# Turning normalised activations channel-major by transposing DMAs in a conv-attention-FFN kernel

## The chip, the cores and the metric
One core of a Trainium2 chip runs the whole program. The metric is device time in microseconds (us), lower is better.

## The reference
The input is 32 images of 192 channels x 1024 positions. Three layers follow each other. Written short:

```
x = x + proj(channel_attention(qkv(x)))        # 8 heads over channels, 192x192 weights, softmax
t = tokens(x)                                  # (32, 1024, 192)
t = t + attention(layernorm(t))                # 6 heads of 32, causal, 1024 x 1024, scale 1/sqrt(192)
t = t + ffn(layernorm(t))                      # two layers, 192 -> 768 -> 192, gelu between
x = image(t)

# ffn: both layers are "bit linear": weights are the sign of (W - mean), by 5 groups of output rows, and
# the layer's output is scaled by its absolute maximum over a group of 6 images (5 groups), times 128, clipped
# to +-(128 - 1e-5). Images 30 and 31 belong to no group: their ffn output is 0.
```

The maximum over six images is why the feed-forward layer goes over a group twice: once to find the maximum, once to use it.

## The kernel before
The program is written with hand-placed semaphores, one instruction list for each engine. Images go in pairs; three pairs make a group of six (GS = 6), and there are five groups and one last pair.

**Front.** `front_part` carries an image through the first layer, the layer norm and the projections to queries, keys and values. Its steps are listed in `STEPS`: xt, g, wg, na, rb, u, mt and t (first layer), z0 to z3 (turn the normalised tokens), qk0 to qk5 and v0 to v3 (projections). A step is a few matmuls into one of two PSUM banks (`FB`) and an evacuation by ScalarE or VectorE. VectorE's layer norm pieces (`layer_norm`: stats, norm, round) are placed by `SMALL_SLOTS`. "round" writes the float16 high part of a half of the tokens (4 tiles of 128) into `zcat`, and POOL writes the low part beside it (L453, semaphore `zlo_made`). So `zcat[:, t, :]` holds, for 128 tokens, 384 float16 values: 192 high and 192 low. The projections need them with channels on the partitions, in `zt`, three blocks of 128 by 1024 tokens. `turn_z` makes this with TensorE: six 128x128 transposes for two token tiles into one PSUM bank (L595), and ScalarE copies the bank to `zt` (L809).

**Attention.** `attention` walks over slots. A slot n takes one tile of 128 queries of one head: scores on TensorE (L616, L618), their maximum on VectorE (L1082), exp on ScalarE (L841), transposes of the probabilities (L630), and later the product with the values. An image has 48 slots. Beside them the front of the next image runs: `SLOTS` says after which slot each step is issued, so z0 stands in slot 31 and qk0 in slot 35 of each image. TensorE, ScalarE and VectorE each follow this order in their own lists, so a wait in a front step holds the slots behind it. The first image's front runs alone, ahead of all attention, and the second image of the last pair has attention with no front beside it.

**SP** loads the next image once step t3 has been read, and then, after qk5, issues 16 DMAs of 192 KB (L374) that lay the high and low parts of queries and keys into `QS` and `KS`. Attention waits for these (`stacked`) at slots 0 and 24 of an image.

**Feed-forward.** `group_tail` runs after three pairs. In its first pass VectorE normalises element b+1 while element b is in work: stats, four maxima of b, norm, round, the other eight maxima (L1109). POOL makes the low parts (L472). TensorE turns them (`turn_z2`, L595, banks `ZP`), ScalarE copies them to `Z2` (`put_z2`, L862), where they stay for the second pass. Then twelve steps (`y1`, L662) multiply a half of 512 tokens by 128 output channels, ScalarE takes the absolute value (L873), VectorE the maximum. `zcat` exists once, so VectorE's round for b+1 must come after the turning of b.

## Time and profile before

| | |
|---|---|
| median of 3 runs | 5051.42 us (5050.09 to 5053.39) |
| profiled execution, its span | 5053.9 us, the time the prediction's sum is made against |
| TensorE busy | 4182.5 us, 83% |
| VectorE busy | 3623.6 us, 72% |
| ScalarE busy | 2966.6 us, 59% |
| GpSimd (POOL) busy | 773.5 us, 15% |
| DMA queue of SP | 154.38 MB, 13.0% of 16 engines' span |

The span is that of one profiled execution, from its first to its last instruction. Busy shares are averages over all stages; busy TensorE time counts modelled ends of pipelined matmuls.

### The profile page before, as it was taken

How to read it: one execution, taken by the hardware profiler on the slowest of the kernel's cores; microseconds unless marked ns; L12 is line 12 of the kernel's file. 1: busy time of each engine (PE TensorE's matmuls, PEld its weight loads, DVE VectorE, ACT ScalarE, POOL GpSimd, SP SyncE). 2: the span in 40 equal slices, each digit the busy share in tenths (PEclk: the TensorE clock that was granted, in tenths of full speed). 3: DMA queues.
4: the chain of work that ended last, by engine and by line, in shares of the span. 5: the costliest groups of instructions: out<-in, count | busy, mean ns of one | idle time of the engine just before them, and what ended most of it. 6: DMA issues, size and time to landing. Idle time of an engine off the chain costs nothing.

```text
span 5053.9 us, 119820 instructions
## 1 busy us (share of the span) xinstructions
PE 4182.5 (83%) x38848; PEld 3015.4 (60%) x38848; DVE 3623.6 (72%) x8151; ACT 2966.6 (59%) x6655; POOL 773.5 (15%) x671
## 2 busy tenths in 40 slices
PE   4989887879889876989897779889876988897777
PEld 2666664556666545666664556666545666664555
DVE  3767678767777786777778667677775777678666
ACT  1555556846555575555566746555575555566745
POOL 0000002600000143000002600000153000002600
PEclk8999998989999998999998989999998999998989
DMA  2111111011121101111111011211101111111011
GB/s 64 33 33 33 34 38 26 0 45 33 38 53 33 33 0 38 33 33 39 33 33 26 0 45 38 46 40 33 33 0 38 33 33 39 33 33 26 0 38 39
DMA packets 46393, 161.72 MB, mean 32 GB/s; under 512 B 10098, under 2 KB 10612, under 8 KB 45684
## 3 DMA queue, kind: packets, MB, share of 16 engines
q1 hardware_dynamic: 45812, 154.38, 13.0%
q8 instruction: 315, 5.16, 0.4%
q14 instruction: 266, 2.18, 0.1%
HBM read 28.52 MB, written 25.17 MB: 11 GB/s over the span
## 4 chain that ended last, share of the span: by engine, by line
issue 78%; POOL 13%; PE 5%; DVE 2%; POOLq 1%; ACT 0%; DMA 0%; SPq 0%; DVEq 0%; ACTq 0%
POOL work L483 7%; POOL hi_z L453 1%; POOL hi_z L472 1%; POOL rstd L448 1%; POOL rstd L468 1%; PE S L662 1%; POOL NK L443 1%; PE OUT L649 1%; PE PT L734 1%; PE PT L630 1%; DVE nmax L1082 0%; PE S L670 0%; DVE work L339 0%; DMA B<-in_b 0%; PE S L616 0%
## 5 line engine op out<-in xcount | busy, mean ns | idle before, releaser
L841 ACT ACTIVATE work<-S,nmax 128x128 f32<-128x128 f32 (+7 forms) x1536 | 1138.8, 742 | 1119.0 <-DVE nmax L1082 1112.1
L1082 DVE TENSOR_REDUCE nmax<-S 128x1 f32<-128x128 f32 (+7 forms) x1536 | 1155.4, 753 | 620.3 <-PE S L618 574.5
L630 PE MATMUL PT<-ident,work 128*128 128x128 f32 x6912 | 1089.2, 282 | 270.5 <-DVE work L339 246.9
L630 PEld LDWEIGHTS PT<-ident,work 128*128 128x128 f32 x6912 | 752.4, 142 | 493.6 <-DVE work L339 291.5
L339 DVE COPY work<-PT 128x512 f32<-128x512 f32 (+3 forms) x1536 | 893.1, 581 | 25.1 <-PE PT L630 19.4
L662 PE MATMUL S<-odd,W1b 128*128 (+1 forms) x2160 | 526.9, 400 | 71.4 <-DVE work L1155 64.1
L483 POOL TENSOR_TENSOR work<-work 128x512 f16<-128x512 f32 x360 | 414.0, 1158 | 148.4 <-ACT work L887 120.1
L662 PEld LDWEIGHTS S<-odd,W1b 128*128 128x128 f16 x2160 | 214.1, 102 | 354.4 <-DVE work L1155 94.8
L616 PE MATMUL S<-KS,QS 128*128 128x512 f16 (+3 forms) x1152 | 335.9, 347 | 103.5 <-issue 60.9
L443 POOL TENSOR_TENSOR NK<-NK,halfneg 96x4 f32<-96x4 f32 x32 | 32.5, 1016 | 2200.7 <-DVE NK L1007 2200.7
L845 ACT ACTIVATE work<-PT 128x512 f32<-128x512 f32 (+3 forms) x768 | 330.3, 430 | 57.1 <-PE PT L630 57.1
L618 PE MATMUL S<-causal,identb 128*128 128x128 bf16 x1536 | 343.9, 224 | 0.0
L616 PE MATMUL S<-odd 128*128 128x512 f16 (+3 forms) x1152 | 315.1, 328 | 9.9 <-ACT work L841 7.1
L895 ACT ACTIVATE work<-work,sc 128x512 f32<-128x512 f32 x360 | 285.7, 801 | 60.9 <-DVE work L1155 60.6
L649 PE MATMUL OUT<-work,odd 128*32 128x128 f32 x6912 | 310.0, 279 | 7.6 <-ACT oT L833 7.6
L649 PE MATMUL OUT<-work,V 128*32 128x128 f32 x6912 | 306.8, 278 | 0.0
L734 PE MATMUL PT<-W2b,work 128*128 128x192 f16 x2880 | 259.5, 252 | 56.0 <-POOL work L483 56.0
L841 ACT ACTIVATION_READ_ACCUMULATOR work<-S,nmax 128x1 f32 x1536 | 299.4, 195 | 0.0
L734 PEld LDWEIGHTS PT<-W2b,work 128*128 128x128 f16 x2880 | 246.9, 101 | 79.2 <-POOL work L483 54.9
L1155 DVE TENSOR_SCALAR work<-S,sc 128x512 f32<-128x512 f32 x360 | 266.5, 801 | 21.6 <-POOL work L483 14.8
L649 PEld LDWEIGHTS OUT<-work,odd 128*32 128x32 f32 x6912 | 239.7, 111 | 51.5 <-issue 33.2
L649 PEld LDWEIGHTS OUT<-work,V 128*32 128x32 f32 x6912 | 237.1, 110 | 41.4 <-issue 33.4
(189 smaller groups left out, 6718.5 us busy)
## 6 DMA issues: line engine op xcount, KB each, us to landing
X<-in_x SPq DMA_DIRECT2D x32, 768.0 KB, 5.3
odd<-hi_z SPq DMA_DIRECT2D x128, 192.0 KB, 4.1
odd<-odd SPq DMA_DIRECT2D x128, 192.0 KB, 4.2
out_y<-work SPq DMA_DIRECT2D x64, 384.0 KB, 3.1
QS<-hi_z SPq DMA_DIRECT2D x64, 192.0 KB, 3.5
QS<-odd SPq DMA_DIRECT2D x64, 192.0 KB, 4.0
KS<-hi_z SPq DMA_DIRECT2D x64, 192.0 KB, 4.6
KS<-odd SPq DMA_DIRECT2D x64, 192.0 KB, 4.5
```

The lines of the kernel that those rows point to most:

```text
L339: copy(PTS[m % 2][:, m // 2 % RING, P * c0:P * (c0 + k)], PT[i % 2][:, 0:P * k]).then_inc(pt_free[i % 2], 1)
L483: pool.tensor_tensor(hs[:, 1, :], H[:, i % MH, :], hs[:, 0, :], ALU.subtract).then_inc(hlo_made, 1)
L616: mm(S[:, n % 2, c0:min(w, c0 + 512)], q, KS[u][:, h, c0:min(w, c0 + 512)], start=True, stop=c0 + 512 < w)
L618: mm(S[:, n % 2, w - P:w], identb[:, :], causal[:, :], start=False, stop=True).then_inc(scores_full, 1)
L630: last = tr(bank[:, P * (j - c0):P * (j - c0) + P], PS[m % 2][:, m // 2 % 2, P * j:P * j + P], ident[:, :])
L649: last = mm(OUT[32 * hh:32 * hh + 32, 0:P], V[u][:, j, D * h:D * h + D], PTS[k % 2][:, unit_of(k, hh) // 2 % RING, P * j:P * j + P], start ...
L662: last = mm(bank, W1b[:, j, P * (i % 6):P * (i % 6) + P], rhs[:, j, :], start=(j == 0), stop=(j == 2))
L734: last = mm(PT[tp % 2][:, C * t:C * t + C], HS[:, hf, part, m, o:o + P], W2b[:, m, :], start=(m == 0 and part == 0), stop=(m == MH - 1 and ...
L841: A(PS[n % 2][:, n // 2 % 2, 0:w], S[:, n % 2, 0:w], ACT.Exp, bias=nmax[:, n:n + 1], accum_out=rowsum[:, n:n + 1]).then_inc(exp_made, 1)
L845: pt_copy(act, lambda o, x: A(o, x, ACT.Copy), pair, i)
L895: A(h, h, ACT.Gelu, bias=rb1[:, i % 6:i % 6 + 1], scale=r1).then_inc(gelu_made, 1)
L1082: v.tensor_reduce(nmax[:, n:n + 1], S[:, n % 2, 0:P * (qtile(n) + 1)], AX.X, ALU.max, negate=True).then_inc(max_made, 1)
```

## The change
The steps z0 to z3 are dropped, with `turn_z`, `turn_z2`, `put_z2` and the float16 identity. Instead SP issues `dma_start_transpose` for each tile of 128 tokens, from `zcat` to `zt` in the front and to `Z2` in the feed-forward, eight per image, in two halves of four that each wait for POOL's low part. A half has its own semaphore (`z_turned`, `z2_turned`), which reaches 64 for each image. TensorE waits for it at qk0 and qk1, and at y1's steps 0 and 6. VectorE waits for both halves ahead of the next element's norm, and its stats no longer wait. The projections and layer norm pieces get other slots: qk and v one later, the layer norm's up to one and a half earlier. `abs_made` starts at 4, which shifts the counts in its waits by 4 and keeps what they stand for.

```diff
--- before.py
+++ after.py
@@ -92,14 +92,14 @@
 
 
 STEPS = ["xt0", "xt1", "xt2", "xt3", "g0", "g1", "wg0", "wg1", "na", "rb", "u", "mt", "t0", "t1", "t2", "t3",
-         "z0", "z1", "z2", "z3", "qk0", "qk1", "qk2", "qk3", "qk4", "qk5", "v0", "v1", "v2", "v3"]
+         "qk0", "qk1", "qk2", "qk3", "qk4", "qk5", "v0", "v1", "v2", "v3"]
 FREES = {"wg0": 2, "wg1": 2, "mt": 2}
 LN_PER = 26
 JR = 8
 XSOFT = 9
 FRONT_STEPS = len(STEPS)
 
-NEEDS = {"g0": "xt3", "wg0": "g1", "na": "wg1", "mt": "u", "t0": "mt", "qk0": "z3"}
+NEEDS = {"g0": "xt3", "wg0": "g1", "na": "wg1", "mt": "u", "t0": "mt"}
 
 
 def bank_of(step):
@@ -118,12 +118,11 @@
 
 
 SLOTS = {"xt0": 0, "xt1": 1, "xt2": 2, "xt3": 4, "g0a": 5, "g0": 6, "g1a": 7, "g1": 8, "wg0": 9, "wg1": 10,
-         "na": 11, "rb": 15, "u": 18, "mt": 19, "t0": 20, "t1": 21, "t2": 22, "t3": 23, "z0": 31, "z1": 32,
-         "z2": 33, "z3": 34, "qk0": 35, "qk1": 36, "qk2": 37, "qk3": 38, "qk4": 39, "qk5": 40, "v0": 41, "v1": 42,
-         "v2": 43, "v3": 44}
-
-SMALL_SLOTS = {"norms": 12, "rdiag": 13, "logits": 16, "xexp": 17, "attn": 17.5, "ln_stats0": 22, "ln_stats1": 25,
-               "ln_norm0": 27, "ln_norm1": 28, "ln_round0": 28.5, "ln_round1": 29}
+         "na": 11, "rb": 15, "u": 18, "mt": 19, "t0": 20, "t1": 21, "t2": 22, "t3": 23, "qk0": 36, "qk1": 37,
+         "qk2": 38, "qk3": 39, "qk4": 40, "qk5": 41, "v0": 42, "v1": 43, "v2": 44, "v3": 45}
+
+SMALL_SLOTS = {"norms": 12, "rdiag": 13, "logits": 16, "xexp": 17, "attn": 17.5, "ln_stats0": 22, "ln_stats1": 24,
+               "ln_norm0": 26, "ln_norm1": 26.5, "ln_round0": 27, "ln_round1": 27.5}
 
 
 def hybrid_kernel(nc, x, wa, wb, wv, wpt, bp, temp, w3, w1, b1, w2, b2, out):
@@ -141,7 +140,6 @@
 
 
         ident = sb("ident", [P, P])
-        ident16 = sb("ident16", [P, P], F16)
         identb = sb("identb", [P, P], BF16)
         causal = sb("causal", [P, P], BF16)
         ones = sb("ones", [CH + 1, CH])
@@ -240,7 +238,6 @@
         FR = ctx.enter_context(nc.psum_tensor("FR", [P, 512], F32))
         FB = [FR[:, :], S[:, 0, 512:1024]]
         Y = [S[:, i // 2, 512 * (i % 2):512 * (i % 2) + 512] for i in range(4)]
-        ZP = [FR[:, :], OUT[:, :]]
 
 
         w_in = sem("w_in")
@@ -259,6 +256,7 @@
         ln_step = sem("ln_step")
         rstd_made = sem("rstd_made")
         zlo_made = sem("zlo_made")
+        z_turned = [sem(f"z_turned{i}") for i in range(2)]
         qkhi_made = sem("qkhi_made")
         qklo_made = sem("qklo_made")
         stacked = [sem(f"stacked{i}") for i in range(2)]
@@ -273,8 +271,7 @@
         ln2_step = sem("ln2_step")
         rstd2_made = sem("rstd2_made")
         z2lo_made = sem("z2lo_made")
-        z2t_full = sem("z2t_full")
-        z2t_made = sem("z2t_made")
+        z2_turned = [sem(f"z2_turned{i}") for i in range(2)]
         y1_full = sem("y1_full")
         abs_made = sem("abs_made")
         max1_step = sem("max1_step")
@@ -366,6 +363,11 @@
                     sp.wait_ge(front_full, after(pair, u, FRONT_STEPS, STEPS.index("t3") + 1))
                     load_x(pair * 2 + (u + 1))
 
+                for hf in range(2):
+                    sp.wait_ge(zlo_made, after(pair, u, 2, hf + 1))
+                    alone(sp)
+                    for t in range(4 * hf, 4 * hf + 4):
+                        sp.dma_start_transpose(zt[:, :, P * t:P * t + P], zcat[:, t, :]).then_inc(z_turned[hf], 16)
 
                 sp.wait_ge(qklo_made, after(pair, u, 6, 6))
                 for grp in range(2):
@@ -389,6 +391,13 @@
                     front(pair, u + 1, True)
 
             def group_tail(g):
+                with sp.Fori(0, GS) as b:
+                    for hf in range(2):
+                        sp.wait_ge(z2lo_made, g * (2 * GS) + b * 2 + (hf + 1))
+                        alone(sp)
+                        for t in range(4):
+                            sp.dma_start_transpose(Z2[:, b, hf, :, P * t:P * t + P],
+                                                   zcat[:, 4 * hf + t, :]).then_inc(z2_turned[hf], 16)
                 with sp.Fori(0, GS) as b:
                     for hf in range(2):
                         store(g * GS + b, hf, g * (2 * GS) + b * 2 + (hf + 3))
@@ -426,7 +435,6 @@
             pool.wait_ge(cst_made, 11)
             pool.affine_select(out=bm, in_=bm, compare_op=ALU.is_ge, fill=MASKED, base=XD - 1,
                                pattern=[[0, 2], [XD, CH // XD], [0, XD]], channel_multiplier=-1).then_inc(cst_made, 1)
-            pool.tensor_copy(ident16[:, :], ident[:, :]).then_inc(cst_made, 1)
             pool.tensor_copy(identb[:, :], ident[:, :]).then_inc(cst_made, 1)
 
             pool.wait_ge(prep, 3)
@@ -493,7 +501,7 @@
         def _(pe):
             mm = nc.tensor.matmul
             tr = nc.tensor.transpose
-            pe.wait_ge(cst_made, 14)
+            pe.wait_ge(cst_made, 13)
             pe.wait_ge(w_in, 16 * 10)
             pe.wait_ge(w_ready, 1)
 
@@ -565,14 +573,11 @@
                         cols = slice((2 * k + t) * P, (2 * k + t + 1) * P)
                         mm(FR[:, C * t:C * t + C], X[0:CH + 1, 0, cols], MT[0:CH + 1, 0, :], start=True, stop=False)
                         last = mm(FR[:, C * t:C * t + C], X[0:CH, 1, cols], MT[0:CH, 1, :], start=False, stop=True)
-                elif name[0] == "z":
-                    k = int(name[1:])
-                    if k % 2 == 0:
-                        pe.wait_ge(zlo_made, after(pair, u, 2, k // 2 + 1))
-                    last = turn_z(FR, k)
                 elif name.startswith("qk"):
                     i = int(name[2:])
                     m, hf = i // 2, i % 2
+                    if m == 0:
+                        pe.wait_ge(z_turned[hf], after(pair, u, 64, 64))
                     for j in range(3):
                         for w in (W3h, W3l):
                             last = mm(FR, w[:, j, P * m:P * m + P], zt[:, j, 512 * hf:512 * hf + 512],
@@ -586,14 +591,6 @@
                                           w[:, j, 2 * C:3 * C], start=(j == 0 and w is W3h),
                                           stop=(j == 2 and w is W3l))
                 last.then_inc(front_full, 1)
-
-            def turn_z(bank, k):
-
-                v = bank.bitcast(F16).rearrange("p (j n) -> p j n", j=4)
-                for t in range(2):
-                    for j in range(3):
-                        last = tr(v[:, j, P * t:P * t + P], zcat[:, 2 * k + t, P * j:P * j + P], ident16[:, :])
-                return last
 
             pe.sem_inc(ot_full, 2)
             pe.sem_inc(y2_full, 4)
@@ -683,34 +680,16 @@
                     pe.wait_ge(st, nb * (GS * STACKS) + STACKS)
                 alone(pe)
 
-                def turn_z2(ab, abs_before):
-                    for k in range(4):
-                        if k % 2 == 0:
-                            pe.wait_ge(z2lo_made, ab * 2 + (k // 2 + 1))
-                        if k >= 2:
-                            pe.wait_ge(z2t_made, ab * 4 + (k - 1))
-                        turn_z(ZP[k % 2], k).then_inc(z2t_full, 1)
-                    if abs_before is not None:
-
-                        pe.wait_ge(abs_made, abs_before)
-                        alone(pe)
-
                 def y1(b, ab):
                     for i in range(12):
                         if i % 6 == 0:
-                            pe.wait_ge(z2t_made, ab * 4 + (2 + 2 * (i // 6)))
-                        if i >= 4:
-                            pe.wait_ge(abs_made, ab * 12 + (i - 3))
+                            pe.wait_ge(z2_turned[i // 6], ab * 64 + 64)
+                        pe.wait_ge(abs_made, ab * 12 + (i + 1))
                         ffn1(Z2[:, b, i // 6], Y[i % 4], i).then_inc(y1_full, 1)
 
-
-                turn_z2(g * GS, None)
-                with pe.Fori(0, GS - 1) as b:
-                    ab = pe.snap(g * GS + b)
-                    y1(b, ab)
-                    turn_z2(pe.snap(ab + 1), ab * 12 + 12)
-                y1(GS - 1, g * GS + (GS - 1))
-                pe.wait_ge(abs_made, nb * (GS * 12))
+                with pe.Fori(0, GS) as b:
+                    y1(b, pe.snap(g * GS + b))
+                pe.wait_ge(abs_made, nb * (GS * 12) + 4)
                 alone(pe)
 
                 def y(b, ab, hf, clips):
@@ -771,6 +750,7 @@
             act.wait_ge(w_ready, 1)
             act.sem_inc(os_made, 2)
             act.sem_inc(hlo_made, MH)
+            act.sem_inc(abs_made, 4)
 
             def front_part(name, pair, u):
                 f = u % 2
@@ -803,10 +783,6 @@
                 elif name[0] == "t":
                     k = int(name[1:])
                     o = A(T0[:, f, 2 * k:2 * k + 2, :], FR[:, 0:2 * C].rearrange("p (a b) -> p a b", a=2), ACT.Copy)
-                elif name[0] == "z":
-                    k = int(name[1:])
-                    v = FR.bitcast(F16).rearrange("p (j n) -> p j n", j=4)
-                    o = A(zt[:, :, 256 * k:256 * k + 256], v[:, 0:3, :], ACT.Copy)
                 elif name.startswith("qk"):
                     i = int(name[2:])
                     A(QKH[:, i // 2, 512 * (i % 2):512 * (i % 2) + 512], FR, ACT.Copy,
@@ -854,14 +830,6 @@
 
             def group_tail(g):
 
-                def put_z2(b, ab):
-                    for k in range(4):
-                        act.wait_ge(z2t_full, ab * 4 + (k + 1))
-                        alone(act)
-                        zv = ZP[k % 2].bitcast(F16).rearrange("p (j n) -> p j n", j=4)
-                        A(Z2[:, b, k // 2, :, 256 * (k % 2):256 * (k % 2) + 256], zv[:, 0:3, :],
-                          ACT.Copy).then_inc(z2t_made, 1)
-
                 def abs_y1(ab):
                     for i in range(12):
                         act.wait_ge(y1_full, ab * 12 + (i + 1))
@@ -872,12 +840,8 @@
                             act.wait_ge(max1_step, ab * 14 + g + (i - JR + 2))
                         A(JUNK[:, i % JR, :], Y[i % 4], ACT.Abs, bias=B1[:, i % 6:i % 6 + 1]).then_inc(abs_made, 1)
 
-                put_z2(0, g * GS)
-                with act.Fori(0, GS - 1) as b:
-                    ab = act.snap(g * GS + b)
-                    abs_y1(ab)
-                    put_z2(act.snap(b + 1), act.snap(ab + 1))
-                abs_y1(g * GS + (GS - 1))
+                with act.Fori(0, GS) as b:
+                    abs_y1(act.snap(g * GS + b))
 
                 def split_h(ab, i):
                     act.wait_ge(gelu_made, ab * 12 + (i + 1))
@@ -966,7 +930,7 @@
                     link(v.scalar_tensor_tensor(out=wbin[:, :, cols], in0=wf[:, :, cols], scalar=means[:, g:g + 1],
                                                 in1=wc[:, :, cols], op0=ALU.is_gt, op1=ALU.subtract))
             dve.wait_ge(prep_all, 3)
-            dve.wait_ge(cst_made, 14)
+            dve.wait_ge(cst_made, 13)
             dve.wait_ge(bias_in, 16)
             v.memset(X[CH:CH + 1, 0, :], 1.0).then_inc(w_ready, 1)
 
@@ -1105,7 +1069,7 @@
 
                 def max_y1(ab, first, last):
                     for i in range(first, last):
-                        dve.wait_ge(abs_made, ab * 12 + (i + 1))
+                        dve.wait_ge(abs_made, ab * 12 + (i + 5))
                         v.tensor_reduce(gm[:, i:i + 1], JUNK[:, i % JR, :], AX.X, ALU.max).then_inc(max1_step, 1)
                     if last == 12:
                         base = ab * 14 + (g + 1)
@@ -1121,10 +1085,11 @@
                     ab = dve.snap(g * GS + b)
                     b1, ab1 = dve.snap(b + 1), dve.snap(ab + 1)
 
-                    dve.wait_ge(z2t_full, ab * 4 + 4)
-                    alone(dve)
                     norm2(b1, ab1, "stats", range(TT))
                     max_y1(ab, 0, 4)
+                    for hf in range(2):
+                        dve.wait_ge(z2_turned[hf], ab * 64 + 64)
+                        alone(dve)
                     norm2(b1, ab1, "norm", range(TT))
                     norm2(b1, ab1, "round", halves[0])
                     norm2(b1, ab1, "round", halves[1])
```

## Rows read from the trace of the kernel before
**Rows 1.** Page, part 1: busy us (share of the span) and instructions of each engine.
```profile
PE 4182.5 (83%) x38848; PEld 3015.4 (60%) x38848; DVE 3623.6 (72%) x8151; ACT 2966.6 (59%) x6655; POOL 773.5 (15%) x671
```

**Rows 2.** Windows: start:end, length, busy time (x instructions) of each engine, PEclk, DMA share, GB/s.
```profile
4910.80:4921.32 10.52, 9.85 (x120) 7.26 (x121) 7.26 (x17) 8.70 (x20) 0.82 (x1) 1.00 0.01 2
5003.14:5012.61 9.47, 7.94 (x94) 5.68 (x95) 7.18 (x18) 6.08 (x16) 0.00 (x0) 1.00 0.01 2
298.70:306.60 7.90, 7.55 (x108) 5.96 (x108) 5.86 (x13) 7.34 (x16) 0.10 (x1) 1.00 0.01 2
283.50:298.70 15.20, 10.29 (x108) 6.77 (x106) 14.39 (x39) 7.60 (x22) 4.92 (x4) 1.00 0.19 53
835.22:849.27 14.05, 11.09 (x60) 5.29 (x60) 13.52 (x41) 9.98 (x15) 5.23 (x5) 0.88 0.00 0
```

**Rows 3.** Timeline of a front in attention: start us, us, engine, line, work.
```profile
293.89 0.55 DVE L991 CAST hi_z<-XT 128x768 f16<-128x768 f32 x1
...
294.53 1.59 POOL L453 TENSOR_TENSOR hi_z<-XT,hi_z 128x768 f16<-128x768 f32 x1 [3.80 <-DVE hi_z L991]
...
298.78 0.51 PE L595 MATMUL FR<-ident,hi_z 128*128 128x128 f16 x6
...
300.09 0.80 ACT L809 ACTIVATE zt<-FR 128x768 f16<-128x768 f16 x1
...
306.79 0.38 PE L578 MATMUL FR<-zt,W3h 128*128 128x512 f16 x1
```

**Rows 4.** Timeline of the first feed-forward pass, one element to the next.
```profile
835.22 3.39 POOL L472 TENSOR_TENSOR hi_z<-XT,hi_z 128x768 f16<-128x768 f32 x2 [3.27 <-DVE hi_z L991]
...
837.11 0.51 PE L595 MATMUL FR<-ident,hi_z 128*128 128x128 f16 x6 [2.92 <-POOL hi_z L472]
...
840.24 9.27 PE L662 MATMUL S<-odd,W1b 128*128 x36
...
841.87 0.69 ACT L873 ACTIVATE work<-S,B 128x512 f32<-128x512 f32 x1 [0.76 <-PE S L662]
...
843.01 7.30 ACT L873 ACTIVATE work<-S,B 128x512 f32<-128x512 f32 x11 [0.45 <-PE S L662]
...
846.32 2.40 DVE L986 TENSOR_SCALAR XT<-T,mv,rstd 128x192 f32 x8
...
849.27 1.84 POOL L472 TENSOR_TENSOR hi_z<-XT,hi_z 128x768 f16<-128x768 f32 x1 [3.27 <-DVE hi_z L991]
```

**Rows 5.** Timeline of POOL and VectorE: first and last element of a group.
```profile
807.52 3.38 POOL L472 TENSOR_TENSOR hi_z<-XT,hi_z 128x768 f16<-128x768 f32 x2 [2.99 <-DVE hi_z L991]
...
877.37 3.39 POOL L472 TENSOR_TENSOR hi_z<-XT,hi_z 128x768 f16<-128x768 f32 x2 [3.27 <-DVE hi_z L991]
...
884.54 7.96 DVE L1109 TENSOR_REDUCE gm<-work 128x1 f32<-128x512 f32 x12 [1.64 <-ACT work L873]
```

**Rows 6.** Timeline of the first front, alone ahead of attention.
```profile
91.77 3.38 POOL L453 TENSOR_TENSOR hi_z<-XT,hi_z 128x768 f16<-128x768 f32 x2 [2.99 <-DVE hi_z L991]
...
100.48 0.63 PE L578 MATMUL S<-zt,W3h 128*128 128x512 f16 x1
```

**Rows 7.** Timeline of SP: first and last stack DMAs, then the next front's first.
```profile
215.85 0.51 SPq L374 DMA_DIRECT2D odd<-hi_z  x1
...
221.91 0.89 SPq L374 DMA_DIRECT2D odd<-hi_z  x1
...
227.32 2.23 SPq L374 DMA_DIRECT2D odd<-odd  x2
...
324.37 0.52 SPq L374 DMA_DIRECT2D QS<-hi_z  x1
```

**Rows 8.** The stack DMAs from hi_z: duration ns min/median/max, and landing us.
```profile
L374 SPq DMA_DIRECT2D odd<-hi_z x128: 513/889/1832, 215.9 to 4947.5; - x128
...
DMA to landing us min/median/max: 2.6/4.2/5.0
```

**Rows 9.** Timeline of TensorE: first scores of slot 48.
```profile
227.26 0.22 PE L616 MATMUL S<-odd 128*128 128x128 f16 x1
```

## Prediction

> **What bounds the kernel now.** I read the page first. TensorE is busy 83% of the span and VectorE 72% [rows 1], an average over two kinds of stage, so the windows come next. In attention with a front running beside it, the stretch that holds the steps z0 to z3 keeps TensorE busy 7.55 and ScalarE 7.34 of 7.90 us, while the layer norm stretch before it is VectorE's (14.39 of 15.20 us) [rows 2]. Work taken from TensorE and ScalarE can therefore pay, but only in the z stretch. The first feed-forward pass, an element of the batch at a time, has VectorE busy 13.52 of 14.05 us [rows 2]: there the reader is to see that neither the PE transposes nor the ScalarE copies set the pace. The timeline shows why: POOL starts the low part of an element's first half at 835.22, TensorE turns it at 837.11, the first feed-forward matmul starts at 840.24, and the next element's low part starts at 849.27 [rows 4].
>
> **Removed.** Per front four steps of six transposes (a group spans 0.51 us on TensorE) and four copies of 0.80 us [rows 3], together 2.0 us of TensorE and 3.2 us of ScalarE, in 32 fronts, of which 31 lie inside attention. What that is worth there I read from the same five slots, 31 to 35, in the last pair: 10.52 us beside a front, 9.47 us where there is none [rows 2]. The 1.05 us between them is all that z0 to z3 and most of qk0 cost, since VectorE's score maxima keep their pace (7.26 against 7.18 us busy). qk0 moves to slot 36 and takes its share with it. Ends: nothing, and the whole 2.0 us of TensorE if the stretch were TensorE's alone. I take 0.8, nearer to the measured pair: 31 x 0.8 = 25 us gained (0 to 62). In the feed-forward pass the same removal gains nothing by itself, as VectorE is the bound; what counts there is the new latency. The dropped identity copy at the start of the program is hidden by the weight loads and costs or gains nothing. The layer norm pieces run one to one and a half slots earlier within VectorE's full stretch: the same work in another order, nothing.
>
> **Added.** Eight transposing DMAs per element, each turning 128 tokens x 384 values (98 KB), issued by SP, four per half, each half after its zlo_made or z2lo_made. Their price is not in this trace. Call d the time from one to the next, and L that from the issue of the last to its landing. The nearest rows are the sixteen stack DMAs of a front: issued from 215.85 to 229.55, 0.86 us each, 192 KB each, the shortest 0.51 us on the queue [rows 7]; they land 2.6 us (shortest) to 4.2 us (median) after issue [rows 8]. A transposing DMA has half the bytes but, in blocks of 128, 384 destination runs of 256 B against 96 of 2 KB. By bytes it would take 0.43 us, which the shortest issue lifts to 0.51; by runs 4 x 0.86 = 3.4; and 4.2 if one had to land before the next. I take twice the stack DMA's pace, d = 1.7, and L = 3.0, as they find the DMA engines empty (DMA share 0.01 [rows 2]). Ends: d 0.51 and 4.2, L 2.6 and 4.2.
>
> The Trainium skill ("VectorE: DVE Perf Modes", The three transpose paths) gives 1309 ns for a 128x128 bf16 block turned by DMA and 390 ns by TensorE; three blocks a DMA would make d an estimated 3.9 and the total about 6100 us. The same skill ("DMA: Bandwidth & Descriptors", Latency and other measured facts) has transposing DMAs at 261 GB/s, by which 98 KB is an estimated 0.38 us of data, and the sum would be near that of the lower end. The rows can't decide between them, as none here transposes by DMA.
>
> **Feed-forward pass, 5 groups of 6 elements.** Counted from the start of an element's first low part: it is ready after 1.84 us [rows 4], its first half is turned at t0 = 1.84 + 3d + L, its second at t1 = 1.84 + 7d + L. zcat has one buffer, and VectorE now waits for both halves before it normalises the next element; ahead of that wait stand four maxima that need the first half's matmuls. From first matmul to the fourth maximum, as now: 840.24, first ScalarE pass 841.87, the next eleven 0.66 apart from 843.01, plus 0.68 for the maximum, 5.5 us [rows 4, 5]. From the start of the normalising to the next low part 2.95 us (846.32 to 849.27) [rows 4]. The period is
> max(t0 + 5.5, t1 + 0.1) + 2.95.
> With d = 1.7 and L = 3.0: t0 = 9.94, t1 = 16.74, period 19.8. Now five periods take 69.85 us (807.52 to 877.37) [rows 5]; after, 99.0. Loss per group 29.1. The last element ends now 15.1 us after its low part begins (877.37 to 884.54 + 7.96) [rows 5]; after, it waits for its second half, then six steps and maxima, 6.2 us: 22.9, a loss of 7.8. Five groups: 5 x 36.9 = 185 us. VectorE's own 13.5 us fits into 19.8; queued behind its wait are the norm, the rounding and eight maxima, so ScalarE and TensorE stand too.
>
> **Attention.** A unit of 48 slots takes 108.5 us (215.85 to 324.37) [rows 7], 2.26 us a slot. Now rounding starts at 293.89 in slot 28.5 and qk0 at 306.79 in slot 35 [rows 3], 12.9 us. After, it is slot 27 to 36, 2.5 slots more, less the 0.8 saved: 17.7 us, and 20.0 to qk1, which needs the second half. Needed from the rounding: 0.64 + 1.59 [rows 3] + 7d + L = 17.1 for qk1, 10.3 for qk0. Both are hidden by the attention of slots 27 to 36; without that cover they would cost their full length. They stay hidden up to d = 2.1. Above it TensorE stands at qk1 with the next scores queued behind it, and VectorE and ScalarE wait for those: 7(d - 2.1) us per front. On SP the stack DMAs come one slot later: now their first half is issued by 221.9 and lands by some 226, and the first scores of slot 48 start at 227.26 [rows 7, 8, 9]. The margin of about 1 us shrinks; 0 to 1 us in 16 units, I take nothing. X's load goes out ahead of the transposes and waits for nothing new.
>
> **The first front** has no cover: from its low part (91.77) to qk1 (100.48) 8.7 us [rows 6]; after, t1 = 16.7, 8 us lost once.
>
> **Sum.** 185 + 8 - 25 = +168 us on the profiled execution's 5053.9 us; that is 2.5 above the median, so from 5051.4: **5219 us**.
>
> **The rivals.**
> (a) Forecast: d from 1.0 to 2.1, hidden in attention, exposed in the feed-forward pass. At d = 1.0 the sum is +54 (5105), at 2.1 +255 (5306). Chance 0.50. For it: VectorE's full loop and the single zcat.
> (b) The transposing DMA is dear, d above 2.1, and holds up attention too. At 2.8: feed-forward +416, first front +16, stalls 31 x 4.9 = 152, less 25: 5610. For it: four times the runs of a stack DMA. Against: half the bytes. Chance 0.17.
> (e) The transposing DMAs do not overlap at all, each waiting for the landing of the one before: d = 4.2 as in [rows 8]. Period 37.3, feed-forward +710, first front +26, stalls 31 x 14.7 = 456, less 25: 6220. Against: the stack DMAs overlap fourfold on the same queue. Chance 0.10. The Trainium skill's 1309 ns a block ("VectorE: DVE Perf Modes", The three transpose paths) would bring the kernel close to this case; no run here shows it yet.
> (c) Faster: the DMAs cost little and the removed work pays more. At d = 0.51 and L = 2.6 the period is 14.4, the last element 16.7, the feed-forward loss 19 us, the first front even; with 0.8 a front the sum is -6, with 2.0 it is -43 (5008). It decides from a gain of 0.6 us a front at that d; at d = 1.0 it would need 2.5, more than the 2.0 that TensorE gives up. For it: the DMA engines are idle. Against: L alone puts 2.6 us where TensorE and ScalarE needed little. Chance 0.12.
> (d) The same balance within 0.2% (10 us), about what a measurement of this kernel can tell from no change: 0.06. The rest, 0.05, goes to losses below (a)'s, d between 0.6 and 1.0.
>
> The range of (a) alone is 5105 to 5306. To hold eight in ten it reaches down into (d) and up to d = 2.8 in (b), and leaves out (e): 5040 to 5610. Faster 0.12, same 0.06, slower 0.82.
>
> **What would show it.** In the first feed-forward pass the low parts on POOL should stand about 20 us apart, with VectorE's XT line waiting for a DMA; SP's transposes give d directly. The wait at the first qk matmuls should stay small; if it is long, (b) holds. Slots 31 to 35 beside a front should come near 9.5 us. The prediction fails if d is far from 1.7, each 0.1 us of it above 1.3 being worth some 21 us, or if transposing DMAs slow the engines' own reads.

## Result: slower by 2.9%, and the profile after

| | before | after |
|---|---|---|
| median | 5052.41 us (5050.09 to 5057.66) | 5198.86 us (5194.31 to 5210.00) |
| ratio, 95% interval | | 1.0293 [1.0278, 1.0308] |
| span of the profiled execution | 5053.9 us | 5194.1 us, 140.2 more |

Times and ratios, here and below, are of fast executions alone: one of experiment 7 (5763.14 us) and one of the kernel before beside experiment 12 (9008.38 us) were slow and are left out.

The page of the changed kernel, part 1 and two lines on its DMAs (packets; the queue SP's DMAs use, with its share of 16 engines' span):

```profile
PE 4112.8 (79%) x37360; PEld 2940.9 (57%) x37360; DVE 3632.8 (70%) x8151; ACT 2791.3 (54%) x6407; POOL 778.8 (15%) x670
...
DMA packets 252727, 210.52 MB, mean 41 GB/s; under 512 B 216434, under 2 KB 216948, under 8 KB 252020
...
q1 hardware_dynamic: 252148, 203.21, 17.5%
```

TensorE and ScalarE have lost the work as intended (ScalarE 2966.6 to 2791.3 us against [rows 1]), yet the span is longer. The transposes bring 206,000 packets under 512 B, but the queue's share is only 17.5%. The engines idle more, so the question is what they wait for.

**The price of a transposing DMA.** Timelines of SP (start, length of the whole burst, count) in the first front and in the feed-forward pass, then the instructions by line (duration in ns min/median/max) with the time from issue to landing:

```profile
93.73 10.38 SPq L370 DMA_TRANSPOSE zt<-hi_z  x8
...
840.39 10.53 SPq L399 DMA_TRANSPOSE odd<-hi_z  x8
```

```profile
L370 SPq DMA_TRANSPOSE zt<-hi_z x256: 1177/1257/2645, 93.7 to 5056.5; - x128
...
L399 SPq DMA_TRANSPOSE odd<-hi_z x240: 1177/1178/1858, 822.9 to 4802.3; - x120
...
DMA to landing us min/median/max: 2.3/2.3/3.6
```

Eight take 10.4 to 10.5 us, so d is 1.30 to 1.32 us (forecast 1.7), and L is 2.3 to 2.4 us (forecast 3.0).

**Feed-forward pass**, one element to the next, timeline of all engines; the answer to [rows 4]:

```profile
838.36 3.38 POOL L480 TENSOR_TENSOR hi_z<-XT,hi_z 128x768 f16<-128x768 f32 x2 [12.23 <-DVE hi_z L955]
...
846.96 9.42 PE L659 MATMUL S<-odd,W1b 128*128 x36 [7.50 <-DMA odd<-hi_z]
...
850.46 2.11 DVE L1073 TENSOR_REDUCE gm<-work 128x1 f32<-128x512 f32 x3 [0.46 <-ACT work L841]
...
852.48 2.40 DVE L950 TENSOR_SCALAR XT<-T,mv,rstd 128x192 f32 x8
...
855.43 3.39 POOL L480 TENSOR_TENSOR hi_z<-XT,hi_z 128x768 f16<-128x768 f32 x2 [6.45 <-DVE hi_z L955]
```

From the low part (838.36) to the first matmul (846.96) are 8.60 us where there were 5.02; the matmuls had waited 7.50 us for the DMA. The fourth maximum ends as the normalising starts (852.48), and 2.95 us later POOL starts the next element. The period is 17.07 us. POOL's first and last element of the group, the answer to [rows 5], and the waits of TensorE for these DMAs in the whole kernel (us in total, times, longest):

```profile
820.87 3.38 POOL L480 TENSOR_TENSOR hi_z<-XT,hi_z 128x768 f16<-128x768 f32 x2 [2.99 <-DVE hi_z L955]
...
906.57 3.39 POOL L480 TENSOR_TENSOR hi_z<-XT,hi_z 128x768 f16<-128x768 f32 x2 [6.47 <-DVE hi_z L955]
```

```profile
PE S L659 <- DMA odd<-hi_z: 278.7, 31, 17.8
```

VectorE, which has a wait of its own for the second half ahead of the normalising, stands there for a DMA once in the whole kernel (from the list of who waited for L399: us, times):

```profile
  DVE XT L950: 0.2, 1
```

So the loop is set by TensorE's wait for the first half and the four maxima behind it, and not by the second half.

Five periods take 85.70 us (69.85 before), and the last element, to 926.1, takes 19.5 us (15.1 before): 20.3 us a group. The whole stretch from a group's last score maximum to the next group's first, by windows, the five stretches summed (first number; then busy time of each engine), is this before and after:

```profile
sum 1368.60, PE 974.17 PEld 619.01 DVE 974.01 ACT 886.58 POOL 574.62; mean PE 194.83 PEld 123.80 DVE 194.80 ACT 177.32 POOL 114.92
```

```profile
sum 1470.56, PE 921.16 PEld 567.52 DVE 981.64 ACT 799.02 POOL 573.79; mean PE 184.23 PEld 113.50 DVE 196.33 ACT 159.80 POOL 114.76
```

That is 102 us more, with VectorE's busy time unchanged (974 and 982): of 140.2 us the largest part is there. Below, this sum is called the group tails. Nearly all of it lies in the first pass: from a group's first low part to its last maximum the five groups together take 526.4 us, where they took 425.6.

**Attention.** The third pair of images by windows that run from one score maximum to another: slot 0, slots 24 to 30 (layer norm), 31 to 35, slot 48 (the second image's first) and slots 72 to 78 (the second image's layer norm). Before, then after:

```profile
575.69:577.31 1.62, 1.62 (x9) 1.06 (x9) 0.29 (x2) 0.84 (x3) 0.00 (x0) 0.50 0.05 15
630.10:644.82 14.72, 9.93 (x106) 6.55 (x104) 13.87 (x38) 7.03 (x22) 4.20 (x4) 1.00 0.22 55
644.82:655.35 10.53, 9.78 (x120) 7.28 (x121) 7.28 (x17) 8.71 (x20) 0.83 (x1) 1.00 0.01 3
683.35:684.24 0.89, 0.85 (x8) 0.39 (x5) 0.89 (x4) 0.49 (x3) 0.00 (x0) 1.00 1.06 221
738.49:752.98 14.49, 9.90 (x106) 6.54 (x104) 13.68 (x39) 7.03 (x22) 4.21 (x4) 1.00 0.22 56
```

```profile
585.91:589.50 3.59, 1.48 (x7) 0.93 (x7) 0.29 (x2) 0.95 (x3) 0.00 (x0) 0.50 0.01 2
642.60:657.77 15.17, 10.95 (x106) 7.14 (x104) 13.84 (x39) 7.14 (x22) 5.24 (x4) 0.89 0.29 66
657.77:667.34 9.57, 8.06 (x95) 5.76 (x96) 7.19 (x17) 6.08 (x16) 0.00 (x0) 1.00 0.33 64
695.76:697.19 1.43, 1.43 (x13) 1.04 (x12) 0.99 (x3) 1.02 (x4) 0.00 (x0) 1.00 0.88 193
751.43:767.34 15.91, 10.92 (x106) 7.41 (x104) 13.84 (x38) 7.23 (x22) 5.22 (x4) 0.89 0.24 58
```

Slots 31 to 35 fall by 0.96 us, as hoped. But slot 0 takes 3.59 instead of 1.62, the layer norm stretches 15.17 and 15.91 instead of 14.72 and 14.49, at a granted clock of 0.89 instead of 1.00, and slot 48 takes 1.43 instead of 0.89. Averaged over the first fifteen pairs (from the start times of the maxima) the first image of a pair takes 110.19 us instead of 108.52 and the second 105.54 instead of 105.09. Over the kernel attention loses about 30 us instead of gaining 25. Three places are to be explained.

*Layer norm.* VectorE and TensorE of the changed kernel in the second image, by timeline, and a window of 2 us in it:

```profile
752.57 1.13 DVE L942 BATCH_NORM_STATS2 stats<-T 128x6 f32<-128x192 f32 x4
753.62 0.41 DVE L946 BATCH_NORM_AGGREGATE mv<-stats 128x2 f32<-128x6 f32 x4
753.95 1.23 DVE L1046 TENSOR_REDUCE nmax<-S 128x1 f32<-128x1024 f32 x1
...
757.37 2.40 DVE L950 TENSOR_SCALAR XT<-T,mv,rstd 128x192 f32<-128x192 f32 x8
...
755.83 0.77 PE L627 MATMUL PT<-ident,work 128*128 128x128 f32 x5 [2.26 <-DVE work L336]
...
761.15 1.12 PE L627 MATMUL PT<-ident,work 128*128 128x128 f32 x4 [2.28 <-DVE work L336]
```

```profile
761.50:763.50 2.00, 2.00 (x11) 0.90 (x9) 1.46 (x5) 1.58 (x5) 1.86 (x2) 0.50 0.02 4
```

Two things have changed in VectorE's order. The second half's statistics (1.13 and 0.41 us), one slot earlier now, stand ahead of a long maximum of 1.23 us. And both halves of the normalising are one piece of 2.40 us, since the new slots 26 and 26.5 meet, again with a long maximum behind it. VectorE's evacuation of the transposed probabilities comes late behind each, and TensorE waits 2.26 and then 2.28 us. After the second wait the granted clock is 0.50, the lower of its two levels (1.2 GHz), in the window from 761.50. In the kernel before the statistics stood ahead of a short maximum, the normalising in two pieces of 1.24 us, and the longest wait of TensorE in that stretch was 1.03 us:

```profile
743.32 0.41 DVE L982 BATCH_NORM_AGGREGATE mv<-stats 128x2 f32<-128x6 f32 x4
743.65 0.29 DVE L1082 TENSOR_REDUCE nmax<-S 128x1 f32<-128x128 f32 x1
...
745.78 1.24 DVE L986 TENSOR_SCALAR XT<-T,mv,rstd 128x192 f32<-128x192 f32 x4
...
750.92 1.06 PE L630 MATMUL PT<-ident,work 128*128 128x128 f32 x8 [1.03 <-DVE work L339]
```

*Slot 48.* Its first scores wait for the stack DMAs ("idle before" in brackets):

```profile
695.45 0.23 PE L613 MATMUL S<-odd 128*128 128x128 f16 x1 [0.82 <-DMA odd<-odd]
```

*Slot 0.* TensorE at the head of the third pair, then the waits of that kind in the whole kernel:

```profile
585.52 0.37 PE L528 MATMUL FR<-ident,X 96*128 96x96 f32 x1
588.02 0.32 PE L527 MATMUL FR<-ident,X 97*128 97x97 f32 x1 [2.13 <-issue]
```

```profile
PE FR L527 <- issue: 29.3, 14, 2.4
```

Between two steps of the front TensorE stands 2.13 us and waits for nothing that the profile shows ("issue"). It does so at 14 of 16 pair heads, 29.3 us in all. The kernel before has no such row: there L519 follows itself without a gap. (Another "issue" wait, ahead of a pair's first scores, is in both kernels, 60.9 us before and 60.8 us after at 14 pairs, and explains no difference.)

### The profile page after: what moved, and what is told of

Its sections match the earlier page's. It is cut to its first block, busy times and chain, and to the rows that moved or that the text cites. A ratio compares the mean times of both kernels' runs of the same rounds, so it can differ in the third digit from the quotient of the medians.

```text
span 5194.1 us, 117149 instructions
## 1 busy us (share of the span) xinstructions
PE 4112.8 (79%) x37360; PEld 2940.9 (57%) x37360; DVE 3632.8 (70%) x8151; ACT 2791.3 (54%) x6407; POOL 778.8 (15%) x670
## 3 DMA queue, kind: packets, MB, share of 16 engines
q1 hardware_dynamic: 252148, 203.21, 17.5%
## 4 chain that ended last, share of the span: by engine, by line
issue 79%; POOL 12%; PE 5%; DVE 2%; DMA 1%; POOLq 1%; SPq 0%; ACT 0%; DVEq 0%; ACTq 0%
POOL work L491 7%; POOL hi_z L461 1%; POOL hi_z L480 1%; POOL rstd L456 1%; POOL rstd L476 1%; PE S L659 1%; PE OUT L646 1%; POOL NK L451 1%; PE PT L627 1%; PE PT L713 1%; DVE nmax L1046 0%; PE S L667 0%; SPq L399 0%; DVE work L336 0%; PE S L613 0%
## 5 line engine op out<-in xcount | busy, mean ns | idle before, releaser
L627 PE MATMUL PT<-ident,work 128*128 128x128 f32 x6912 | 1104.0, 284 | 286.0 <-DVE work L336 271.7
L659 PE MATMUL S<-odd,W1b 128*128 (+1 forms) x2160 | 545.5, 410 | 350.4 <-DMA odd<-hi_z 278.7
L613 PE MATMUL S<-KS,QS 128*128 128x512 f16 (+3 forms) x1152 | 340.8, 352 | 97.2 <-issue 60.8
L841 ACT ACTIVATE work<-S,B 128x512 f32<-128x512 f32 x360 | 238.4, 687 | 332.6 <-PE S L659 329.3
L1073 DVE TENSOR_REDUCE gm<-work 128x1 f32<-128x512 f32 x360 | 228.1, 680 | 131.8 <-ACT work L841 130.3
```

What stands on the lines that cost most here:

```text
L613: mm(S[:, n % 2, c0:min(w, c0 + 512)], q, KS[u][:, h, c0:min(w, c0 + 512)], start=True, stop=c0 + 512 < w)
L627: last = tr(bank[:, P * (j - c0):P * (j - c0) + P], PS[m % 2][:, m // 2 % 2, P * j:P * j + P], ident[:, :])
L659: last = mm(bank, W1b[:, j, P * (i % 6):P * (i % 6) + P], rhs[:, j, :], start=(j == 0), stop=(j == 2))
```

## Experiments

The ratios are to the kernel before, measured in turn with it. The edits are shown shortened: "..." marks what is left out, semaphore counts are left out too, and the comments in them are mine.

**1. The front alone** (feed-forward pass as before) and **2. the feed-forward pass alone** (front as before). Edits: the hunks of the diff for the one part, the other left out.

> The front's transposes go by DMA with the changed slots, the feed-forward pass keeps TensorE and ScalarE. Theory A (the loss is the sum of two stages: 102 us in the five feed-forward gaps, 5 us in the first front, some 33 us in attention): 5052 + 38 = 5090 us. Theory B (attention loses only because the feed-forward pass hands its images over late or with a slow TensorE clock): 5052 + 5 - 25 = 5032 us.

Measured: 5090.77 us, ratio 1.0074 [1.0058, 1.0091]; group tails 1374.9 us, images 110.00 and 105.45 us.

> Only the feed-forward pass turns by DMA, the front is the old one. Theory A: 5052 + 102 = 5154 us, low parts on POOL 17.1 us apart, pairs as long as before. Theory B: some 33 us more, 5187 us, as the pairs grow with it.

Measured: 5155.90 us, ratio 1.0204 [1.0187, 1.0221]; group tails 1469.5 us, images 108.31 and 105.07 us. The parts add up (39 + 104 us, against the 146 us of both together), and the front costs time though it was meant to save it.

**3. The layer norm's and projections' old slots.**

```diff
-SLOTS = {..., "qk0": 36, "qk1": 37, ..., "v3": 45}
+SLOTS = {..., "qk0": 35, "qk1": 36, ..., "v3": 44}
-"ln_stats1": 24, "ln_norm0": 26, "ln_norm1": 26.5, "ln_round0": 27, "ln_round1": 27.5
+"ln_stats1": 25, "ln_norm0": 27, "ln_norm1": 28, "ln_round0": 28.5, "ln_round1": 29
```

> The changed kernel with the layer norm pieces back in the slots of before and qk and v one slot earlier again. Theory A1 (attention loses by the new slots: 0.7 to 1.0 us a unit in slots 24 to 30, and 0.6 to 0.8 us at slot 48, where the scores wait for late stack DMAs): slots 24 to 30 back at 14.6 us, no wait at slot 48, 26 + 11 us gained, 5199 - 37 = 5162 us. Theory A2 (the transposing DMAs in flight slow the engines, whatever the slots): no gain, or a loss of up to 2 us a front where qk1 now waits for its half, 5199 to 5260 us.

Measured: 5187.07 us, ratio 1.0262 [1.0245, 1.0279]. Slots 24 to 30 are back at 14.76 and 14.49 us and slot 48 at 0.95, as expected. The total is not, 25 us above theory A1: qk0 in slot 35 gives back 0.6 us of each 0.96, TensorE waits at qk1 for the second half's DMAs in five images (6.9 us in all), and the group tails are 13 us longer (1483.5), though nothing was edited there. Of these 13, 5 lie in the first pass (531.8 against 526.4) and 6 behind it. That part I can't explain.

**4. Code moved.** 64 instructions without work on TensorE's list, ahead of its loop over the groups; nothing else.

```diff
+            for _ in range(64):
+                alone(pe)
             groups(pe, pair_body, group_tail)
```

> The changed kernel with 64 semaphore increments more on TensorE, once, ahead of its loops: no work in any loop changes, only where the loop's instructions lie in memory. Theory C (the 2.0 us more in the first slot of each pair are a wait for TensorE's instructions, set by where the code lies): the first slot's 3.6 us change, to some 1.5 us or to more, and the whole by up to 15 x 2 = 30 us either way. Theory D (the wait has to do with the changed work): nothing changes, 5199 us.

Measured: 5175.53 us, ratio 1.0240 [1.0223, 1.0257]. Slot 0 falls from 3.55 to 1.57 us on average; slots 24 to 30 rise by 0.4 to 0.5 us. The 64 instructions run once, ahead of the loop, so what changes inside it is only where TensorE's code lies, and the wait at slot 0 depends on that. The 0.4 to 0.5 us given back in slots 24 to 30 are not explained.

**5. Two buffers in the feed-forward pass.** `zt` is free there and serves as a second `zcat`. VectorE normalises an element ahead, and its wait is for the transposes of the element before last. With the buffer VectorE's order changes too: the normalising moves ahead of the four maxima, and the loops over elements are written out.

```diff
+        zcat2 = [zcat, zt[:, :, :].rearrange(...)]
...
-                            sp.dma_start_transpose(Z2[...], zcat[:, 4 * hf + t, :])
+                            sp.dma_start_transpose(Z2[...], zcat2[b % 2][:, 4 * hf + t, :])
...
+                norm2(0, ..., "stats"); normalise(0); norm2(1, ..., "stats")
+                for b in range(GS):
+                    if b + 1 < GS: normalise(b + 1)       # waits for the transposes of b - 1
+                    max_y1(b, 0, 4)
+                    if b + 2 < GS: norm2(b + 2, ..., "stats")
+                    max_y1(b, 4, 12)
```

> The changed kernel with a second zcat (in zt, idle in the feed-forward pass), VectorE normalising element b+1 ahead of the maxima of b, and only waiting for the turning of b-1. Theory A (the 102 us are the DMAs' latency inside VectorE's loop, not their work): the loop falls back to VectorE's own 13.6 us a period, the last element ends some 8 us after its first maximum; 105 us per group become 80, 5199 - 5 x 25 = 5074 us. Theory B (eight transposing DMAs and their SP issue are a bound of their own, or slow the engines): period near 17 us stays, no gain over 20 us.

Measured: 5100.10 us, ratio 1.0097 [1.0080, 1.0114]. The group tails fall from 1470.6 to 1378.8 us, 92 us of the 125 expected, and the whole kernel stays 26 us above the expectation. POOL's third and sixth element of a group in this kernel:

```profile
847.78 3.38 POOL L482 TENSOR_TENSOR hi_z<-XT,hi_z 128x768 f16<-128x768 f32 x2 [6.44 <-DVE hi_z L957]
...
889.12 3.39 POOL L482 TENSOR_TENSOR zt<-XT,zt 128x768 f16<-128x768 f32 x2 [6.36 <-DVE zt L957]
```

The period is 13.8 us ((889.12 - 847.78) / 3), a little under the 13.97 of before, with the same eight DMAs an element. From first low part to last maximum the five groups take 427.9 us, against 526.4 in the changed kernel and 425.6 before. So what the DMAs cost in the changed kernel was latency in a loop with one buffer, and neither SP's time nor the transfers. A group's first element still waits uncovered, but the 10 us by which the tails stay above those of before lie mostly behind the first pass (8 us), and no run says why.

**6. The same with the layer norm's old slots** (third and fourth line of experiment 3's diff alone).

> As the pipelined kernel, and the layer norm pieces in the slots of before (qk and v stay one slot later). Slots 24 to 30 back to 14.6 us and 31 to 35 at 9.57, so 0.7 to 1.0 us a unit less than the pipelined one: 5074 - 26 = 5048 us, level with before's 5052 or just under it. If the layer norm slots were not the cause in attention, 5074 us.

Measured: 5084.99 us, ratio 1.0063 [1.0046, 1.0080], 15 us less than experiment 5 and 37 more than expected: the 26 of experiment 5, gaps between the pairs that grew by 6.6 us, and group tails that grew by 4.8. The layer norm stretch of the last pair (slots 24 to 30), after and in this kernel:

```profile
5034.39:5050.48 16.09, 10.96 (x106) 7.40 (x104) 13.80 (x39) 7.21 (x22) 5.28 (x4) 0.89 0.07 13
```

```profile
4929.80:4944.04 14.24, 9.82 (x106) 6.50 (x104) 13.70 (x39) 7.02 (x22) 4.25 (x4) 1.00 0.04 7
```

1.85 us less, clock 1.00: the slots of the layer norm alone bring the stretch back, while the projections keep their later ones. The clock itself seems to cost little there: in experiment 9 below, slots 24 to 30 of the third pair have 0.88 and take 14.82 us. So it is mostly the waits that cost. The experiment moves all the pieces back at once, so it does not tell the merged normalising from the statistics ahead of a long maximum.

**7. One DMA of twelve blocks a half** in place of four of three, and **8. one block a DMA**, both with the single `zcat`. In 7 `Z2` is laid out by token tiles and TensorE reads it in four pieces of 128.

```diff
-                        for t in range(4):
-                            sp.dma_start_transpose(Z2[:, b, hf, :, P * t:P * t + P], zcat[:, 4 * hf + t, :])
+                        sp.dma_start_transpose(Z2[:, b, hf, :, :, :].rearrange("p t j n -> p (t j) n"),   # 7
+                                               zcat[:, 4 * hf:4 * hf + 4, :])
...
+                            for j in range(3):                                                           # 8
+                                sp.dma_start_transpose(Z2[:, b, hf, j, P * t:P * t + P],
+                                                       zcat[:, 4 * hf + t, P * j:P * j + P])
```

> The changed kernel with one transposing DMA for each half in the feed-forward pass (12 blocks of 128x128) in place of four of 3 blocks; Z2 is laid out so that its output is contiguous, and the matmuls read it in four runs of 128. Theory A (SP pays by block, 0.43 us): a half still takes 5.2 us and lands 2.4 us later at most, period 17 us or up to 1 us more, 5199 us or up to 25 more. Theory B (SP pays by instruction, some 1.2 us): a half lands within 3 us, the period falls to VectorE's 14 us, 5199 - 90 = 5109 us.

> The changed kernel with three transposing DMAs of one 128x128 block each in place of one of three blocks, in the feed-forward pass. Theory A (by block): SP issues one in 0.43 us, 1.3 us a tile of tokens as now, 5199 us. Theory B (by instruction): 1.2 us each, 3.6 a tile, period 1.8 + 23 x 1.2 + 2.4 + 3.0 = 35 us, 5 x 5 x 18 + 5 x 16 = 530 us more, 5730 us.

Measured: 7 takes 5134.62 us, ratio 1.0170 [1.0149, 1.0190], 26 above its expectation, tails 1415.4; 8 takes 5810.37 us in one execution, 80 above, tails 2083.6. The instructions by line and their landing, first of 7, then of 8, and SP's burst for one element in each (two and 24 instructions):

```profile
L398 SPq DMA_TRANSPOSE odd<-hi_z x60: 1420/1504/1618, 821.6 to 4738.7; - x60
...
DMA to landing us min/median/max: 3.7/3.8/3.9
...
852.14 3.27 SPq L398 DMA_TRANSPOSE odd<-hi_z  x2
```

```profile
L400 SPq DMA_TRANSPOSE odd<-hi_z x720: 1093/1142/1868, 825.0 to 5418.9; - x180
...
DMA to landing us min/median/max: 2.2/2.3/3.7
...
862.68 30.52 SPq L400 DMA_TRANSPOSE odd<-hi_z  x24
```

Twelve blocks cost 1.50 us of SP, three 1.18 to 1.26, one 1.14: nearly all of the price is that of the instruction. A burst of 24 takes 1.27 us each. In experiment 8 the second half's matmuls start 33.95 us after the low part and the period is 36.9, so there the prediction's other branch decides, t1 and then 2.95 us; VectorE's XT line waits for these DMAs 25 times, 230.7 us in all. In experiment 7 the period is 15.1 on average (between POOL's low parts at 819.57 and 895.00) where the formula gives 14.4 for the measured t0 of 6.0. The five periods run from 14.4 to 15.7 us. In the longest but one, 15.6, the first four steps and maxima take 6.65 us instead of 5.5, with ScalarE's passes 1.28 us apart (858.91, 860.19, 861.47), each waiting for TensorE. Windows of that element and of one with a period of 14.4, both 3.86 us after its first matmul, show the reason: the granted clock (third number from the end) is 0.50 in the one and 1.00 in the other:

```profile
860.00:862.00 2.00, 2.00 (x6) 0.70 (x5) 1.00 (x2) 1.22 (x2) 0.71 (x1) 0.50 0.00 0
890.46:892.46 2.00, 2.00 (x11) 0.88 (x9) 1.98 (x5) 2.00 (x4) 0.70 (x1) 1.00 0.00 0
```

TensorE had waited 5.16 and 5.17 us before the two, and what decides how long the clock stays low is not shown. The Trainium skill ("VectorE: DVE Perf Modes", The three transpose paths) gives 1309 ns for a 128x128 bf16 block by DMA. The runs agree with it for a DMA of one block (1.27 us from one to the next), but it is no price per block: with twelve in one DMA a block takes 0.14 us (3.27 / 24).

**9 to 11. The three cures together, the same with code moved, and the control.** 9: two buffers, one DMA a half, the layer norm's old slots. 10: 9 with experiment 4's 64 instructions. 11: the kernel before with them.

> The kernel with two buffers and before's layer norm slots (e6, 5085 us), and in the feed-forward pass one DMA of twelve blocks a half instead of four of three. Theory A (the latency that is left is that of a group's first element and the wait for the second half): the first half is turned 2.5 us earlier by the runs so far (3 x 1.3 + 2.4 against 3.8), the second 3.8 us earlier, so the five group tails fall from 1384 to about 1365 and the kernel comes to 5067 us. Rival B (TensorE reading the tokens in four pieces of 128 is slower, or the single DMA disturbs the engines): the tails stay at 1384 or rise, 5085 us or more.

Measured: 5056.90 us, ratio 1.0016 [1.0007, 1.0025], group tails 1359.2 us. Theory A holds, at 10 us less than it gave; the tails are now 9 us shorter than before's, the first pass in them 20 us (405.8 against 425.6).

> The same with 64 instructions without work on TensorE's list ahead of the loop over groups, which shifts all later code. Theory C (the first slots of a pair wait for instructions, by where the code lies): slot 0 of a pair falls by about 2 us in 16 pairs, 23 to 32 us less if nothing is given back elsewhere (5040 us), about 11 less if half is given back as in the run padded before (5056 us). Rival: the same time as without the padding (5067 us), if that run's gain was by chance.

Measured: 5022.62 us, ratio 0.9954 [0.9940, 0.9968], 34 us less than experiment 9. By the traces slots 0 and 1 of 15 pairs give 25 us of it and slot 48, whose wait for the stack DMAs is gone too, 7. Waits of TensorE for "issue" in the transposing steps of 9; in 10 the list has no such row. Then the window of slot 0 of the third pair in 9 and in 10:

```profile
PE FR L528 <- issue: 31.1, 14, 2.4
...
582.93:587.11 4.18, 1.77 (x9) 1.08 (x8) 0.29 (x2) 0.95 (x3) 0.00 (x0) 0.50 0.01 2
```

```profile
581.51:582.81 1.30, 1.30 (x7) 0.74 (x7) 0.29 (x1) 0.84 (x3) 0.00 (x0) 0.50 0.03 6
```

> The kernel before with the same 64 instructions without work ahead of TensorE's loop over groups, the control. Theory C: before's TensorE shows no wait for instructions at the head of a pair, so shifting its code can only bring such waits or leave it: 5051 to 5080 us. Rival: the padding helps any kernel (by timing at the start of a pair, not by place): about 5030 us.

Measured: 5055.04 us, ratio 1.0011 [1.0002, 1.0020]. The padding takes 34 us from one kernel and adds 5 to the other, so it is no help in itself; it moves code out of an unlucky place. Some 3 us of the 5 may be the 64 instructions themselves, run once: the first scores of all come after a wait of 9.09 us instead of 6.26. In experiment 10 nothing was given back in slots 24 to 30, unlike in experiment 4.

**12. Is the DMA worth anything in the front?** Experiment 10 with the kernel before's front.

> The best kernel so far (two buffers, one DMA a half, before's layer norm slots, 64 instructions ahead, 5022.6 us) with the front put back to TensorE's transposes and ScalarE's copies: what the transposing DMAs are worth in the front alone. Theory A (worth the 0.96 us of slots 31 to 35 in each image, against 5.6 us lost in the first front): by the traces of the two padded kernels an image with it takes 0.72 to 0.98 us less, 27 us over 32 images, so without it 5022.6 + 27 - 6 = 5044 us. Rival B: the gain over the padded kernel before came from the two buffers and the one DMA in the feed-forward pass, and the front is even: 5023 us.

Measured: 5037.08 us, ratio 0.9974 [0.9965, 0.9983]. Theory A's direction, at half its size: the ratios of experiments 10 and 12 differ by 0.0020, 10 us, the medians by 14. The two intervals just touch, so the direction is likely and the size is not known well. The spans differ by 13.5: 28 less in attention for the DMAs, 5.7 lost in the first front, 3.0 in the gaps between pairs, and tails 5.8 us longer (1356.0 against 1350.2), which the theory did not have. The first pass takes 404.6 us in both, so these 5.8 are not of the feed-forward DMAs. Against experiment 11 the feed-forward part alone takes 20 us off the tails (1370.4 to 1350.2).

## Why the prediction was right, and where its terms were off

The forecast was slower, 5219 us; it came to 5198.86, by the mechanism of its case (a): the DMAs are exposed in the feed-forward pass and hidden in attention. But its terms were further off than the sum, and two errors cancelled. That the total came within 20 us is luck.

- **The formula of the feed-forward period held.** With d = 1.32 and L = 2.3 it gives t0 = 8.1 and a period of 16.6; measured 8.6 and 17.07 (0.5 us more from low part to first matmul), and the 5.5 and 2.95 us came as put. But it is not the branch that was forecast. At d = 1.7 the second half's turning (t1 + 0.1 = 16.8) would have decided, with VectorE waiting for a DMA; below d = 1.35 it is the first half and the four maxima (t0 + 5.5). So the announced sign, VectorE's XT line waiting for a DMA, did not show (0.2 us, once), and the low parts stand 17.1 us apart and not 20. The branch of the forecast held in experiment 8, and the cost of the loop fell away with the second buffer (experiment 5), as a latency must.
- **The size of d and L was off**: 1.7 and 3.0 against 1.30 to 1.32 and 2.3 to 2.4. So the term of +185 us came to +102; the formula itself gives +87 for the measured d and L. The step that failed was taking "twice the stack DMA's pace" for four times the runs at half the bytes. Neither is the measure: SP's time per instruction, about 1.3 us from one to the next, is (experiments 7 and 8).
- **The first front**: forecast +8. From low part (91.80) to qk1 (105.34) are now 13.5 us instead of 8.7, and the first score maximum comes 5.5 us later, in line with the smaller d and L.
- **Slots 31 to 35** came to 9.57 us, the 9.5 of the prediction. Nothing waits at qk0 or qk1 in attention, as forecast for d under 2.1. That part of the gain, 0.96 x 31 = 30 us, is real, and experiment 12 is in line with it.
- **"The same work in another order, nothing"** is the step that failed outright. Statistics came to stand ahead of a long maximum, two pieces of 1.24 us became one of 2.40, and TensorE waited 2.3 us twice. Experiment 6 shows the slots as the cause: by the image means of experiments 5 and 6, 0.60 and 0.89 us, 24 us over 32 images (15 in the medians). In the changed kernel slots 24 to 30 had grown by 0.71 and 0.98 us on average, 27 us in all.
- **The margin of the stack DMAs** was known to shrink and taken at nothing. Slot 48 grew by 0.44 us on average. The wait is gone with the old slots of the projections (experiment 3), but also in experiments 4 and 10, which have the later slots and moved code (0.7 and 0.2 us in the whole kernel). Every kernel with the later slots and the wait at slot 0 has 9.3 to 10.6 us of it, so the two seem to go together; what links them stays open.
- **Slot 0** was not in the prediction at all: 3.55 instead of 1.54 us on average, of which slot 1 gives back 0.54: some 23 us. Experiments 4 and 10 show that it goes with the place of TensorE's code, and experiment 11 that the padding alone gains nothing. That the engine waits for its own instructions to be fetched is my reading of "issue" waits that moved; no run measured the fetch.

With d and L as measured the forecast would have been +87 + 5 - 25 = +67, or 5118 us: 80 too low. Of that some 15 us are in the group tails, mostly the half microsecond more from low part to first matmul, and 55 are in attention. The overpriced DMA made up for the costs that were missing, the layer norm slots and slots 0 and 48. Rival (c), faster, came out only after the kernel was rebuilt around the DMAs, at 5022.62 us (experiment 10), and by half a per cent.

In us against the kernel before, the measured ones from the profiled spans:

| | forecast | measured |
|---|---|---|
| group tails | +185 | +102.0 |
| first front | +8 | +5.5 |
| attention, 32 images | -25 | about +30 |
| the rest (gaps between pairs, end) | 0 | about +2 |

## What to carry to other kernels

When work moves from an engine to a DMA, count the latency first: in a loop with one buffer it is paid in full, and a second buffer, with VectorE's order fitted to it, removed 92 us of 102. Pay transposing DMAs by the instruction and put as many blocks into one as the layout allows. Pieces on a shared engine that "only" move a slot can merge, or come to stand ahead of another long one, and starve a neighbour, so look at the longest run of work between two hand-overs and not at the sum; and before a difference of some 0.5% is put down to an edit, move the code and measure again.

## What the runs showed of the hardware

- A transposing DMA costs SP 1.14, 1.18 to 1.26 and 1.50 us for one, three and twelve 128x128 blocks of 2-byte values, and lands 2.3, 2.3 to 2.4 and 3.8 us after issue.
- 64 instructions without work on TensorE's list changed a kernel by 34 us (5056.90 to 5022.62) and another by 23 (5198.86 to 5175.53), for the most part through waits of up to 2.4 us that the profile puts down to "issue". A third kernel, without such waits, became 5 us slower (5049.96 to 5055.04).
- TensorE's granted clock stayed 1.00 after one wait of 2.26 us and was 0.50 after a second of 2.28 us, 5.3 us later.
- After waits of 5.16 and 5.17 us in one loop TensorE's granted clock was still 0.50 in one case and 1.00 in the other, 3.86 us into its work, and that round of the loop took 15.6 and 14.4 us.
